# Two attention stages of a decoder kernel: context keys and values projected in parts, and self-attention on units of 256 queries

## The chip, the cores and the metric

The kernel runs on one core of a Trainium2 chip. The metric is the device time of one execution, in microseconds, the median of several runs.

## The reference

The computation is a stack of 12 blocks on x of shape (4 batches, 256 tokens, 128 channels). Two of them matter here.

The second context attention (layer 1): 16 heads of 8 channels, 256 queries per batch, keys and values projected from a context of 1601 places with 96 channels, a different one for each of the 4 batches. In float32: q = LN(x) Wq + bq, scaled by 8^-0.5; k = c Wk + bk; v = c Wv (its bias is added behind). The scores less their row maximum are clamped to +-10000, the softmax is over the 1601 places, and the result times Wo is added to x.

The non-causal self-attention inside layer 2's feed-forward block: a convolution over tokens, then 16 heads of 8 channels over the 256 tokens of a batch, softmax over all 256 keys, no mask.

## The kernel before, in words

Each stage of the program has one program of its own for each engine, ordered by hand; they meet on semaphores. The tensor engine takes its matmuls in program order. All arrays are float32, and each float32 matmul stands in the trace as two instructions. The 8 PSUM banks hold 512 float32 columns each.

**Second context attention** (`attend_clipped`, L1449; called from `layer1_context`, L1700). The work is cut into 16 units, a batch b and a group g of four heads, `X_UNITS` (L1387). A unit has 13 ticks, one for each tile of 128 context places (`JT`). For its queries a unit needs first the row maxima. `scan` (L1493) makes all scores in 11 bursts of three matmuls of 401 columns into banks 0 to 2; `reduce_` (L1640) on the vector engine takes the maxima of a burst. `prepare` (L1646) gathers and clamps them, `turn` (L1513) transposes them on the tensor engine into banks 0 and 1, and `add` (L1654) puts them into the queries. Then `fill` (L1519) makes the scores again, transposed and shifted, for a pair of ticks, in banks 3 to 6; ScalarE's `take` (L1586) makes the exponentials (L1611); `clip` (L1662) on the vector engine clips each tick against a floor; `values` (L1544) sums into bank 7, and ScalarE's `copy` (L1615) takes that out at the end of the unit.

The stage is pipelined over units (`SCAN_FROM`, L1390, and `bursts_in`, L1393). At ticks 0 to 5 of unit u the last six bursts of unit u + 1 are scanned and reduced, at ticks 8 to 12 the first five of unit u + 2. Ticks 6 and 7 have no burst. The vector engine gathers unit u + 1 at tick 6 and adds at tick 8 (L1677 to L1689); at tick 7 in the third unit of a batch it also sums the next context (`context_sum`, L1669).

Banks 3 to 6 are handed on by one chain of slots (`slots_in`, L1403; `X_SLOTS`). Each slot is filled by the tensor engine when ScalarE has taken the slot before (semaphores `filled` and `taken`). Slots are pairs, one floor per unit (tick 9), and, at tick 7 (`PREPARE_AT`) of the first two units of batches 0 to 2, the keys and the values of the next batch: four matmuls of up to 512 columns for keys (L1526), thirteen of 128 columns for values (L1529). ScalarE takes keys in one instruction into `k_rows` (L1594), values in two (L1601, L1602).

The queue of SP (L1471) spreads the keys by 16 DMAs from `k_rows` to `kT`, which is double-buffered by batch, and loads the contexts of batches 2 and 3. Its order is: two groups of the first keys, load 2, spread 1, load 3, spread 2, spread 3. Each waits for a count of `taken`, load also for the sum of an earlier context.

The order of the tensor engine at a tick, from the tick loop:

```python
for m in bursts_in(n):
    scan(m)
if i == PREPARE_AT and u + 1 < U:
    turn(u + 1)
for slot in slots_in(n):
    fill(slot)
if n == PAIRS[PAIR[n]][-1]:
    values(PAIR[n])
```

**Non-causal self-attention** (`self_attention`, L392, with causal=False, called at L2939). A unit is a batch, a group of four heads and one tile of 128 queries: 32 units. For each: `scan` (L438, four matmuls of 256 columns at L456, banks 0 to 3), `reduce` (L537, 1024 columns at L542), `turn` (L482, one transpose at L487, spare columns of bank 0), `shift` (L545, L552), `score` (L459, eight matmuls of 128 columns at L478, banks 4 to 7), one exponential of 1024 columns (L528), `values` (L490, eight matmuls of 128 columns at L496, spare columns of bank 4), and ScalarE's copy (L531). The order on the tensor engine is scan u + 1, score u, turn u + 1, values u. A scan waits for the shift of the unit before, a score for the copy of the unit before. The causal form of the same function, in other layers (L0a below is one), already has units of 256 queries, two exponentials of 768 columns per unit (L526), and the order score u, scan u + 2, turn u + 1, values u. When all units are through, 32 transposes (L516) and the division by the sums follow.

## Time and profile before

| | |
|---|---|
| median of 3 runs | 4305.74 us |
| lowest, highest | 4303.53, 4313.3 us |
| the profiled execution's own time | 4302.7 us |
| its span in the profile | 4301.0 us |
| mean granted TensorE clock | 0.873 of 2.4 GHz |
| tensor engine (PE) busy | 3334.1 us, 78% |
| vector engine (DVE) busy | 2990.1 us, 70% |
| ScalarE (ACT) busy | 1872.6 us, 44% |
| GpSimd (POOL) busy | 352.4 us, 8% |
| DMA queues | 5.1% of 16 engines' span |

The profile is of one execution, with times from the start of its span. A row of its timeline gives the start, the duration, the engine (PEld is the weight load of the tensor engine), the line of the kernel, the operation, what it writes and reads (partitions x elements), how many instructions were merged, and in brackets the idle time of the engine before it and what ended that. Busy shares over the whole span are means over many stages with different limits, so a stage is read by itself. The granted clock is a share of 2.4 GHz; 0.50 is 1.2 GHz.

### The profile page before, as it was taken

What the parts mean: (1) busy time and instruction counts of PE and PEld (TensorE: products, weight loads), DVE (VectorE), ACT (ScalarE), POOL (GpSimd) and SP (SyncE); (2) the same over time, 40 slices, a digit from 0 to 9 for tenths busy, and PEclk for the clock granted to TensorE, in tenths of its full rate; (3) what the DMA queues carried; (4) which work ended last, traced back from release to release, by engine and by line L of the source; (5) the groups of instructions that cost most, each with busy time, mean ns of one, the idle gap of its engine ahead of it and who ended that gap; (6) DMA issues with size and microseconds to landing.
All of it is one profiled execution on the core that took longest, in us unless ns stands there. A gap on an engine that the chain in (4) does not pass through costs nothing. (4 is left out here: it accounts for less than half of the span.)

```text
span 4301.0 us, 59641 instructions
## 1 busy us (share of the span) xinstructions
PE 3334.1 (78%) x24338; PEld 1735.1 (40%) x24338; DVE 2990.1 (70%) x4102; ACT 1872.6 (44%) x2168; POOL 352.4 (8%) x150
## 2 busy tenths in 40 slices
PE   5799999999999955877776884466654669477579
PEld 3433333333333324333334653223322347344357
DVE  4577777777777776699896446699998454546642
ACT  2365555565555532344442233344442236244233
POOL 0000000000000000000000000044441000000000
PEclk9899999999999978799997997666566789688789
DMA  2000000000000000100002001000000100010010
GB/s 83 9 15 8 8 15 8 8 13 10 8 8 15 1 12 13 22 8 8 9 1 94 30 2 47 1 0 0 0 0 0 41 11 30 9 40 1 1 41 6
DMA packets 21604, 68.51 MB, mean 16 GB/s; under 512 B 5201, under 2 KB 5713, under 8 KB 20434
## 3 DMA queue, kind: packets, MB, share of 16 engines
q1 hardware_dynamic: 21330, 64.69, 5.1%
q8 instruction: 193, 3.16, 0.3%
q14 instruction: 81, 0.66, 0.0%
HBM read 49.07 MB, written 0.52 MB: 12 GB/s over the span
## 5 line engine op out<-in xcount | busy, mean ns | idle before, releaser
L1071 PE MATMUL banks<-L0x_ring,L0x_context_rows 128*101 128x512 f32 x1600 | 734.7, 602 | 4.0 <-ACT L0x_ring L1119 4.0
L1130 ACT COPY L0x_ring<-banks 128x1024 f32<-128x1024 f32 (+1 forms) x416 | 387.1, 982 | 533.9 <-PE banks L1059 533.9
L1059 PE MATMUL banks<-L0x_q_thirds,L0x_context_thirds 32*128 32x512 f32 x4800 | 593.8, 606 | 10.3 <-DVE L0x_q_thirds L1236 5.3
L1161 DVE TENSOR_TENSOR L0x_ring<-L0x_ring,L0x_greatest 128x2048 f32<-128x2048 f32 (+1 forms) x208 | 469.9, 2268 | 10.9 <-ACT L0x_ring L1130 9.4
L1177 DVE TENSOR_TENSOR L0x_maxima<-L0x_maxima,L0x_ring 128x1024 f32<-128x1024 f32 (+1 forms) x288 | 322.8, 1162 | 201.1 <-ACT L0x_ring L1130 200.9
L1071 PEld LDWEIGHTS banks<-L0x_ring,L0x_context_rows 128*101 128x101 f32 x1600 | 253.9, 167 | 456.0 <-issue 448.9
L1119 ACT ACTIVATE L0x_ring<-L0x_ring 128x2048 f32<-128x2048 f32 (+1 forms) x208 | 386.4, 1858 | 16.6 <-DVE L0x_ring L1161 16.2
L1059 PEld LDWEIGHTS banks<-L0x_q_thirds,L0x_context_thirds 32*128 32x128 f32 x4800 | 237.1, 185 | 347.0 <-issue 306.7
L1611 ACT ACTIVATE L1x_probs<-banks 128x2048 f32<-128x2048 f32 (+1 forms) x112 | 196.6, 1755 | 252.6 <-PE banks L1540 210.8
L1644 DVE TENSOR_REDUCE L1x_maxima<-banks 128x3 f32<-128x1203 f32 (+1 forms) x176 | 241.3, 1372 | 54.1 <-PE banks L1509 54.1
L1667 DVE SCALAR_TENSOR_TENSOR L1x_probs<-L1x_probs,L1x_floor 128x1024 f32<-128x1024 f32 (+1 forms) x208 | 252.1, 1216 | 13.0 <-ACT L1x_probs L1611 13.0
L1509 PE MATMUL banks<-L1x_k,L1x_q 32*128 32x401 f32 x1024 | 176.8, 579 | 92.2 <-DVE L1x_maxima L1644 87.7
L1266 POOL PARTITION_ALL_REDUCE L0x_greatest<-L0x_folded_maxima x32 | 93.7, 2928 | 1388.5 <-DVE L0x_folded_maxima L1194 720.5
L3414 PE MATMUL banks<-L2x_k,L2x_q_of_head 128*128 128x512 f32 (+1 forms) x256 | 183.9, 813 | 0.0
L3519 DVE MAX8 L2x_top<-L2x_rest 128x8 f32<-128x1601 f32 x96 | 175.6, 1829 | 3.3
L3524 DVE MATCH_REPLACE8 L2x_rest<-L2x_top,L2x_rest 128x1601 f32<-128x1601 f32 x96 | 173.9, 1812 | 0.0
L1540 PE MATMUL banks<-L1x_q_shifted,L1x_k 32*128 32x256 f32 (+1 forms) x1664 | 169.7, 397 | 4.0 <-ACT L1x_probs L1611 4.0
L1177 DVE TENSOR_TENSOR L0x_maxima<-L0x_ring 128x1024 f32<-128x1024 f32 x64 | 75.6, 1222 | 97.1 <-ACT L0x_ring L1130 97.1
L3487 POOL TENSOR_TENSOR L2x_exp_all<-L2x_exp_all,L2x_exp_rest 128x1601 f32<-128x1601 f32 x31 | 110.9, 3577 | 258.6 <-ACT L2x_exp_top L3477 258.6
L1509 PEld LDWEIGHTS banks<-L1x_k,L1x_q 32*128 32x128 f32 x1024 | 56.8, 193 | 176.0 <-DVE L1x_maxima L1644 158.6
L1540 PEld LDWEIGHTS banks<-L1x_q_shifted,L1x_k 32*128 32x128 f32 (+1 forms) x1664 | 108.1, 185 | 35.5 <-ACT L1x_probs L1611 14.6
L250 PE MATMUL banks<-identity,z_rows 128*128 128x128 f32 x96 | 25.1, 438 | 125.1 <-DVE z_rows L285 123.7
(948 smaller groups left out, 5272.2 us busy)
## 6 DMA issues: line engine op xcount, KB each, us to landing
L0x_q_thirds<-L0x_q_context SPq DMA_DIRECT2D x180, 64.0 KB, 2.0
L1f_expert_weights<-in_L1f_experts SPq DMA_DIRECT2D x16, 512.0 KB, 10.0
L2f_expert_weights<-in_L2f_experts SPq DMA_DIRECT2D x8, 512.0 KB, 4.9
L3a_expert_weights<-in_L3a_experts SPq DMA_DIRECT2D x8, 512.0 KB, 5.6
L3f_expert_weights<-in_L3f_experts SPq DMA_DIRECT2D x8, 512.0 KB, 6.6
L1x_k<-L1x_k_rows SPq DMA_DIRECT2D x64, 50.0 KB
L0x_context_thirds<-in_context_thirds SPq DMA_DIRECT2D x1, 2496.0 KB, 14.3
L1x_context<-in_context SPq DMA_DIRECT2D x4, 600.4 KB, 4.7
```

Source lines behind the costliest of these rows:

```text
L1059: mm = pe.matmul(k.ps[:, score_bank(s) + i, :], thirds[group_rows(i), slot, t, :], q_thirds[group_rows(i), u // 2 % 2, t, :], start=t == 0 ...
L1071: mm = pe.matmul(k.ps[0:CW, bank, :], rows1[0:height(j), j, :], ring[0:height(j), s % RING, i, :], start=s == FIRST[u] and i == 0, stop=s ...
L1119: act.activation(ring[:, s % RING, 0:len(js), :], ring[:, s % RING, 0:len(js), :], ACT.Exp).then_inc(exped, 1)
L1130: act.copy(ring[0:r, s % RING, 2 * p:2 * p + len(pair), :], k.ps[0:r, bank:bank + len(pair), :]).then_inc(copied, 1)
L1161: dve.tensor_tensor(o, o, greatest[:, u % 2, None, :].broadcast_to([P, len(js), 512]), ALU.subtract).then_inc(shifted, 1)
L1177: dve.tensor_tensor(o, before, ring[0:r, s % RING, 2 * p:2 * p + m, :], ALU.max).then_inc(maxed, 1)
L1509: mm = pe.matmul(k.ps[:, bank + i, 0:WIDE], qT[row(h), g, b * S + it * P:b * S + (it + 1) * P], kT[row(h), b % 2, g, 400 * c:400 * c + WID ...
L1540: mm = pe.matmul(k.ps[0:height(j), 3 + h, i * S:(i + 1) * S], kT[row(h), b % 2, g, j * P:j * P + height(j)], qs[row(h), u % 2, :], start=T ...
L1611: act.activation(probs[0:r, at % 2, 0:m, :].rearrange("p a (h q) -> p h a q", h=4), k.ps[0:r, 3:7, 0:m * S].rearrange("p h (a q) -> p h a ...
L1644: dve.tensor_reduce(mx[:, u % 2, items[0]:items[-1] + 1], k.ps[:, scan_bank(m):scan_bank(m) + len(items), 0:WIDE], X, ALU.max).then_inc(re ...
L1667: dve.scalar_tensor_tensor(out=o, in0=o, scalar=1.0, in1=floor[0:height(j), u % 2, :], op0=ALU.min, op1=ALU.max).then_inc(clipped, 1)
L3414: mm = pe.matmul(k.ps[:, i, 0:m], qh[:, h, b * S + it * P:b * S + (it + 1) * P], kT[:, b % 2, c:c + m], start=False, stop=True)
```

## The change

It has two parts.

In the second context attention the slots of keys and values for batches 1 to 3 are gone. In their place each of the first 12 units has one part at tick 6: `part_ahead` on the tensor engine, into scan banks 1 and 2, and `take_part` on ScalarE. For the next batch, the first unit of a batch does the keys of places 0 to 801, the second those of 801 to 1600 (place 801 twice), the third the values of eight tiles, the fourth those of five. The part waits for all reductions of the next unit; the first scan of the next unit but one waits for `part_taken`. The turn now uses bank 0 alone. The gather stays at tick 6. SP's spread and load wait for counts of `part_taken`: the spread for the second part of a batch, load 3 for the fourth.

In layer 2 a new function, `attend_whole_batches`, takes the place of the non-causal call. Its units are 16, a batch and a group with all 256 queries. Exponentials are two of 1024 columns into a single buffer; a scan waits only for the reduction of the unit before, and the order on the tensor engine is that of the causal form.

The diff, cut where lines repeat what stands here:

```diff
+def attend_whole_batches(k, ctx_name, qT, kT, v, y, heads, dv):
+
+    groups = heads // 4
+    units = [(b, g) for b in range(B) for g in range(groups)]
+    U = len(units)
+    with ExitStack() as ctx:
+        low = k.sb(ctx_name + "_minus_max", [P, 2, TPB, P], ctx=ctx)
+        qs = k.sb(ctx_name + "_q_shifted", [P, 2, S], ctx=ctx)
+        probs = k.sb(ctx_name + "_probs", [P, 4, TPB * S], ctx=ctx)
+        yT = k.sb(ctx_name + "_y_columns", [P, TILES, groups, P], ctx=ctx)
+        rden = k.sb(ctx_name + "_reciprocal_sums", [P, TILES, heads], ctx=ctx)
+        with k.stage() as (block, signal):
...
+            @block.tensor
+            def _(pe):
+                def scan(u):
+                    if u:
+                        pe.wait_ge(reduced, u)
+                    for it in range(TPB):
+                        for h in range(4):
+                            mm = pe.matmul(k.ps[:, h, whole(it)], queries(u)[row(h), tile(it)], keys(u)[row(h)], start=True, stop=True)
+                    mm.then_inc(scanned, 1)
+
+                def turn(u):
+                    pe.wait_ge(reduced, u + 1)
+                    if u:
+                        pe.wait_ge(exped, 2 * u - 1)
+                    for it in range(TPB):
+                        mm = pe.transpose(k.ps[:, 6, tile(it)], low[:, u % 2, it, :], k.ident[:])
+                    mm.then_inc(turned, 1)
+
+                def score(u):
+                    pe.wait_ge(shifted, u + 1)
+                    if u:
+                        pe.wait_ge(copied, u)
+                    for j in range(TPB):
+                        for h in range(4):
+                            mm = pe.matmul(k.ps[:, 4 + h, whole(j)], keys(u)[row(h), tile(j)], qs[row(h), u % 2, :], start=True, stop=True)
+                    mm.then_inc(scored, 1)
+
+                def values(u):
+                    b, g = units[u]
+                    pe.wait_ge(exped, 2 * u + 2)
+                    for j in range(TPB):
+                        for h in range(4):
+                            mm = pe.matmul(k.ps[row(h), 4, 0:S], v[:, b * TPB + j, 4 * g + h, :], probs[:, h, whole(j)],
+                                           start=j == 0, stop=j == TPB - 1)
+                    mm.then_inc(summed, 1)
+
+                scan(0)
+                turn(0)
+                scan(1)
+                for u in range(U):
+                    score(u)
+                    if u + 2 < U:
+                        scan(u + 2)
+                    if u + 1 < U:
+                        turn(u + 1)
+                    values(u)
+                pe.wait_ge(copied, U)
...
+            @block.scalar
+            def _(act):
+                for u, (b, g) in enumerate(units):
+                    act.wait_ge(scored, u + 1)
+                    act.activation(probs[:, 2:4], k.ps[:, 6:8, :], ACT.Exp).then_inc(exped, 1)
+                    act.activation(probs[:, 0:2], k.ps[:, 4:6, :], ACT.Exp).then_inc(exped, 1)
+                    act.wait_ge(summed, u + 1)
+                    act.copy(yT[:, b * TPB:(b + 1) * TPB, g, :], k.ps[:, 4, 0:S].rearrange("p (t j) -> p t j", t=TPB)).then_inc(copied, 1)
+
+            @block.vector
...
+                def reduce(u):
+                    dve.wait_ge(scanned, u + 1)
+                    if u >= 2:
+                        dve.wait_ge(turned, u - 1)
+                    dve.tensor_reduce(low[:, u % 2, :, 31::32], k.ps[:, 0:4, :].rearrange("p h (i n) -> p i h n", i=TPB), X, ALU.max,
+                                      negate=True).then_inc(reduced, 1)
+
+                def shift(u):
+                    dve.wait_ge(turned, u + 1)
+                    if u >= 2:
+                        dve.wait_ge(scored, u - 1)
+                    dve.tensor_tensor(qs[:, u % 2, :], queries(u), k.ps[:, 6, 0:S], ALU.add).then_inc(shifted, 1)
+
+                reduce(0)
+                for u in range(U):
+                    shift(u)
+                    if u + 1 < U:
+                        reduce(u + 1)
...
@@ -1387,7 +1510,10 @@
 X_UNITS = [(b, g) for b in range(B) for g in range(4)]
 TICKS = JT * len(X_UNITS)
 NB = len(BURSTS)
-SCAN_FROM, GATHER_AT, PREPARE_AT, ADD_AT, FLOOR_AT = -5, 6, 7, 8, 9
+SCAN_FROM, PART_AT, GATHER_AT, PREPARE_AT, ADD_AT, FLOOR_AT = -5, 6, 6, 7, 8, 9
+PARTS_AHEAD = 4 * (B - 1)
+KEY_PARTS = ((0, 401), (801, 400))
+VALUE_PARTS = (range(0, 8), range(8, JT))
 
 
 def bursts_in(n):
@@ -1403,10 +1529,7 @@
 def slots_in(n):
 
     u, i = divmod(n, JT)
-    b, g = X_UNITS[u]
     out = []
-    if b + 1 < B and g < 2 and i == PREPARE_AT:
-        out.append(("values" if g else "keys", b + 1))
     if i == FLOOR_AT and u + 1 < len(X_UNITS):
         out.append(("floor", u + 1))
     out += [("pair", p) for p, tiles in enumerate(PAIRS) if tiles[0] == n + 2]
...
             def spread(b):
-                sp.wait_ge(taken, SLOT[("keys", b)] + 1)
+                sp.wait_ge(part_taken, 4 * (b - 1) + 2)
                 if b == 1:
...
             def load(b):
-                sp.wait_ge(taken, SLOT[("values", b - 2)] + 1)
+                if b == 2:
+                    sp.wait_ge(taken, SLOT[("values", 0)] + 1)
+                else:
+                    sp.wait_ge(part_taken, 4 * (b - 2))
                 sp.wait_ge(summed_context, b - 1)
                 sp.dma_start(context[:, b % 2, :], k.dram["context"][b]).then_inc(arrived[b], 16)
...
                 if burst == 0 and u:
                     pe.wait_ge(shifted, u)
+                if burst == 0 and 2 <= u < PARTS_AHEAD + 2:
+                    pe.wait_ge(part_taken, u - 1)
...
             def turn(u):
                 pe.wait_ge(clamped, u + 1)
                 for it in range(TPB):
-                    mm = pe.transpose(k.ps[:, it, 0:P], low[:, u % 2, it, :], k.ident[:])
+                    mm = pe.transpose(k.ps[:, 0, it * P:(it + 1) * P], low[:, u % 2, it, :], k.ident[:])
                 mm.then_inc(turned, 1)
+
+            def part_ahead(u):
+                b, g = X_UNITS[u]
+                pe.wait_ge(arrived[b + 1], 16)
+                pe.wait_ge(reduced, NB * (u + 2))
+                if g < 2:
+                    at, width = KEY_PARTS[g]
+                    for i in range(2):
+                        mm = pe.matmul(k.ps[:, 1 + i, 0:width], w["k"], context[:, (b + 1) % 2, at + i * width:at + (i + 1) * width],
+                                       start=True, stop=True)
+                else:
+                    for i, j in enumerate(VALUE_PARTS[g - 2]):
+                        mm = pe.matmul(k.ps[0:height(j), 1 + i // 4, i % 4 * P:(i % 4 + 1) * P],
+                                       context[:, (b + 1) % 2, j * P:j * P + height(j)], w["v"], start=True, stop=True)
+                mm.then_inc(part_made, 1)
 
...
@@ -1547,7 +1686,10 @@
                     b, g = X_UNITS[u]
                     pe.wait_ge(clipped, n + 1)
                     if j == 0:
-                        pe.wait_ge(taken, SLOT[("values", b)] + 1)
+                        if b:
+                            pe.wait_ge(part_taken, 4 * b)
+                        else:
+                            pe.wait_ge(taken, SLOT[("values", 0)] + 1)
                         if u:
                             pe.wait_ge(copied, u)
...
@@ -1573,6 +1715,8 @@
                     turn(u + 1)
                 for slot in slots_in(n):
                     fill(slot)
+                if i == PART_AT and u < PARTS_AHEAD:
+                    part_ahead(u)
                 if n == PAIRS[PAIR[n]][-1]:
                     values(PAIR[n])
             pe.wait_ge(copied, U)
...
+            def take_part(u):
+                b, g = X_UNITS[u]
+                at = b + 1
+                if g == 0:
+                    for i in range(G):
+                        act.wait_ge(first_keys.here[i], 64)
+                    if b:
+                        act.wait_ge(spread_keys, 16 * H * b)
+                if g == 2:
+                    if at == 1:
+                        act.wait_ge(cleared, 4)
+                    else:
+                        act.wait_ge(summed, PAIR[JT * G * (at - 1) - 1] + 1)
+                act.wait_ge(part_made, u + 1)
+                if g < 2:
+                    first, width = KEY_PARTS[g]
+                    act.activation(k_rows[:, first:first + 2 * width].rearrange("p (a n) -> p a n", a=2), k.ps[:, 1:3, 0:width],
+                                   ACT.Identity, bias=w["bk"]).then_inc(part_taken, 1)
+                elif g == 2:
+                    act.copy(v[:, at % 2, 0:8, :, 0:d], k.ps[:, 1:3, :].rearrange("p a (j h e) -> p (a j) h e", h=H, e=d)).then_inc(part_taken, 1)
+                else:
+                    act.copy(v[:, at % 2, 8:JT - 1, :, 0:d], k.ps[:, 1, :].rearrange("p (j h e) -> p j h e", h=H, e=d))
+                    act.copy(v[0:JLAST, at % 2, JT - 1, :, 0:d], k.ps[0:JLAST, 2, 0:P].rearrange("p (h e) -> p h e", h=H)).then_inc(part_taken, 1)
+
...
@@ -1657,7 +1817,7 @@
                 if u >= 2:
                     dve.wait_ge(taken, SLOT[("pair", PAIR[JT * (u - 1) - 1])] + 1)
                 dve.tensor_tensor(qs[:, u % 2, :].rearrange("p (t j) -> p t j", t=TPB),
-                                  qT[:, g, b * S:(b + 1) * S].rearrange("p (t j) -> p t j", t=TPB), k.ps[:, 0:TPB, 0:P], ALU.add).then_inc(shifted, 1)
+                                  qT[:, g, b * S:(b + 1) * S].rearrange("p (t j) -> p t j", t=TPB), k.ps[:, 0, 0:S].rearrange("p (t j) -> p t j", t=TPB), ALU.add).then_inc(shifted, 1)
...
@@ -2936,7 +3096,7 @@
-            self_attention(k, "L2f", q, kk, v, y, H, d, causal=False)
+            attend_whole_batches(k, "L2f", q, kk, v, y, H, d)
```

## Rows read from the trace of the kernel before

**Rows 1.** Windows, plain unit: length; PE, PEld, DVE, ACT, POOL busy; PEclk; DMA
```profile
1895.30:1926.00 30.70, 23.88 (x282) 11.76 (x282) 29.80 (x28) 14.29 (x16) 0.00 (x0) 1.00 0.01 1
```

**Rows 2.** Timeline, vector engine: the gathers that begin the prepare of each unit
```profile
1791.74 0.20 DVE L1648 TENSOR_REDUCE L1x_unit_maxima<-L1x_maxima 128x8 f32<-128x32 f32 x1
1828.13 0.20 DVE L1648 TENSOR_REDUCE L1x_unit_maxima<-L1x_maxima 128x8 f32<-128x32 f32 x1
1862.97 0.20 DVE L1648 TENSOR_REDUCE L1x_unit_maxima<-L1x_maxima 128x8 f32<-128x32 f32 x1
1895.26 0.20 DVE L1648 TENSOR_REDUCE L1x_unit_maxima<-L1x_maxima 128x8 f32<-128x32 f32 x1
1926.01 0.20 DVE L1648 TENSOR_REDUCE L1x_unit_maxima<-L1x_maxima 128x8 f32<-128x32 f32 x1
1960.69 0.20 DVE L1648 TENSOR_REDUCE L1x_unit_maxima<-L1x_maxima 128x8 f32<-128x32 f32 x1
1995.54 0.20 DVE L1648 TENSOR_REDUCE L1x_unit_maxima<-L1x_maxima 128x8 f32<-128x32 f32 x1
...
2029.43 0.20 DVE L1648 TENSOR_REDUCE L1x_unit_maxima<-L1x_maxima 128x8 f32<-128x32 f32 x1
...
2163.64 0.20 DVE L1648 TENSOR_REDUCE L1x_unit_maxima<-L1x_maxima 128x8 f32<-128x32 f32 x1
```

**Rows 3.** Timeline, all engines: a slot of keys (from 1928) and one of values
```profile
1928.07 3.01 PE L1526 MATMUL banks<-L1x_context,L_weights 96*128 96x512 f32 x8 [1.16 <-ACT L1x_probs L1611]
...
1931.01 1.06 PE L1554 MATMUL banks<-L1x_probs,L1x_v 128*16 128x256 f32 x16
1931.12 1.60 ACT L1594 ACTIVATE L1x_k_rows<-banks,L_weights 128x1601 f32<-128x1601 f32 x1 [3.10 <-PE banks L1526]
...
1933.00 1.41 DVE L1644 TENSOR_REDUCE L1x_maxima<-banks 128x3 f32<-128x1203 f32 x1 [3.73 <-PE banks L1509]
...
1962.76 3.16 PE L1529 MATMUL banks<-L_weights,L1x_context 96*128 96x128 f32 x26 [1.16 <-ACT L1x_probs L1611]
```

**Rows 4.** Timeline, all engines: ticks 6 to 8 of a plain unit
```profile
1894.08 1.15 PE L1540 MATMUL banks<-L1x_q_shifted,L1x_k 32*128 32x256 f32 x16
...
1895.30 1.88 ACT L1611 ACTIVATE L1x_probs<-banks 128x2048 f32<-128x2048 f32 x1 [1.68 <-PE banks L1540]
...
1895.72 0.44 PE L1516 MATMUL banks<-identity,L1x_minus_max 128*128 128x128 f32 x2 [0.49 <-DVE L1x_minus_max L1652]
...
1897.40 0.61 PE L1509 MATMUL banks<-L1x_k,L1x_q 32*128 32x401 f32 x3
...
1898.44 1.41 DVE L1644 TENSOR_REDUCE L1x_maxima<-banks 128x3 f32<-128x1203 f32 x1
```

**Rows 5.** Timeline, ScalarE: one unit of the non-causal loop at the full clock
```profile
3500.56 1.02 ACT L528 ACTIVATE L2f_probs<-banks 128x1024 f32<-128x1024 f32 x1 [0.93 <-PE banks L478]
...
3502.35 0.27 ACT L531 COPY L2f_y_columns<-banks 128x128 f32<-128x128 f32 x1 [0.76 <-PE banks L496]
...
3503.54 1.02 ACT L528 ACTIVATE L2f_probs<-banks 128x1024 f32<-128x1024 f32 x1 [0.93 <-PE banks L478]
```

**Rows 6.** Timeline, ScalarE: two exponentials of the same loop in its beginning
```profile
3417.57 1.02 ACT L528 ACTIVATE L2f_probs<-banks 128x1024 f32<-128x1024 f32 x1 [1.76 <-PE banks L478]
...
3421.81 1.02 ACT L528 ACTIVATE L2f_probs<-banks 128x1024 f32<-128x1024 f32 x1 [1.76 <-PE banks L478]
```

**Rows 7.** Timeline: exponentials, values and copy of one unit of a causal loop
```profile
81.08 1.51 ACT L526 ACTIVATE L0a_probs<-banks 128x768 f32<-128x768 f32 x2 [1.39 <-PE banks L474]
...
82.74 0.86 PE L496 MATMUL banks<-L0a_probs,L_v 128*32 128x128 f32 x24
...
83.67 0.37 ACT L531 COPY L0a_y_columns<-banks 128x256 f32<-128x256 f32 x1 [1.07 <-PE banks L496]
```

**Rows 8.** Windows: two stretches of the non-causal loop
```profile
3414.00:3418.00 4.00, 3.33 (x42) 2.25 (x41) 1.51 (x2) 1.04 (x3) 0.00 (x0) 0.50 0.00 0
...
3446.00:3458.00 12.00, 8.78 (x172) 5.57 (x164) 6.06 (x8) 5.16 (x8) 0.00 (x0) 1.00 0.01 2
```

52 lines of the change are left out of this document (33 added, 19 removed).

## The prediction

> **What bounds the kernel now.** I read the page first (the tensor engine is busy 78% of the span, the vector engine 70%), but the change touches only two stages, so the answer has to come from those. The second context attention runs from about 1735 to 2295 us, the loop of the non-causal self-attention from 3409 to 3512 us. For each I read the timeline of one repeating unit, then the same engines where the pattern breaks.
>
> In the second context attention a unit is 13 ticks. The windows view of a plain unit shows the vector engine busy 29.80 of 30.7 us at full granted clock [rows 1]: it bounds the plain unit. The start of the gather of maxima, one per unit, gives the period [rows 2]: 30.75 us plain (1895.26 to 1926.01), 32.29 where the sum of a context is taken (a 1.54 us longer unit), 36.39 and 34.68 with a projection of keys, 34.84 and 34.85 with one of values. So the projections are no longer covered: in such a slot the tensor engine waits for the exponentials, writes all four score banks for 3.0 to 3.2 us, ScalarE empties them, and only then the next pair and the next scan can start; the vector engine stands idle 3.73 us before a reduction [rows 3].
>
> In the self-attention no engine is full. The exponentials of neighbouring units start 2.98 us apart at the full clock [rows 5], and 4.24 us apart while the granted clock is 0.50 [rows 6, 8]. This is a ring: scores, exponential, values, copy, and the next scan and scores queued behind. The reader should see it in the 1.02 us exponential that fills only a third of the period.
>
> **Part 1, the projections leave the score banks.** Removed are six slots. Their price over a plain unit, from [rows 2]: 5.64 (36.39 - 30.75), 4.09, 3.93 and 4.10; for the last batch 2029.43 to 2163.64 is 134.21 us, less four plain units (123.00) and one context sum (1.54), leaves 9.67. Sum 27.43 us.
>
> Added are twelve parts, one in each of the first twelve units, at tick 6, behind the fill of the pair of ticks 8 and 9 and ahead of the turn of the next unit. In the plain unit that fill ends at 1895.23 and the turn starts at 1895.72 [rows 4]. The part also waits for the last reduction of the next unit; on the vector engine this lies ahead of a 1.2 us clip and of the gather at 1895.26, so it is over by 1894.1 and costs nothing. If it were late, the turn and the values of ticks 6 and 7 would be late behind it.
>
> A part of keys is 802 columns; 1601 take 3.01 us [rows 3], so 1.5 us. The turn then ends near 1897.2 instead of 1896.16, and the values of ticks 6 and 7 (0.98 us of issue) end near 1898.1. ScalarE is in the exponential until 1897.18 and its read-out until 1897.26 [rows 4], so the projection is done when it comes to it; 802 columns of its copy cost about 0.87 us (1.60 us for 1601 and 0.37 for 256 [rows 3, 7]). The banks are free at 1898.2, and the first scan of the next unit but one, queued behind, starts there and not at 1897.40: 0.8 us late, and the reduction of 1898.44, which had no wait, with it. A full vector engine cannot win that back. The second part of values (ten instructions of 26 that take 3.16 us, 1.2 us, then two short copies, 0.86 us) comes to 0.8 as well. The first part of values (1.9 us, a copy of about 1.1) falls into the unit in which the vector engine sums a context for 1.8 us at just this place; the next scan waits for that: 0, and 1.0 if the cover failed. That is 9 x 0.8 = 7.2 us. Bounds: nothing per part, or the whole of its projection and copy in a row (1.5 + 0.9 for keys; 1.9 + 1.1 and 1.2 + 0.9 for values: 9.9 a batch, 30 in all). I take 7.2 since the rows around it fix both starts. **Gain of part 1: 20.2 us**, from 27 to -3.
>
> Edits that cost nothing: both transposes of a turn go to one bank and the add reads one bank (same columns). The spread of keys leaves SP's queue a unit later than before; its 16 DMAs need about 11 us of issue, and the first scan that needs them comes a unit (31 us) after. Behind it on SP stand the load of context 3, now some 30 us later but wanted five units on, and the next spread. The cover for both is one unit; without it the first scan of a batch waits.
>
> **Part 2, units of 256 queries.** 32 units become 16. Tensor work is the same in columns: scan and scores are 16 instructions of 256 columns each, the form that takes 1.15 us for 16 [rows 4], values 16 at 1.06 [rows 3], the turn 0.44. The new ring, from the start of the scores: 1.21 to the first exponential (1894.08 to 1895.30); two exponentials of 1024, 1.95 us, as the causal loop runs two of 768 in 1.51, overlapping by 0.1 [rows 7]; 0.05 to values; 1.12 to the copy; 0.37 of copy; 0.1 to the next scores. 4.8 to 4.9, I take 4.85. The other ring, turn 0.44, add 0.4, reduction of 2048 (2.4, scaling 1.41 for 1203), scan 1.0, is about 4.3 and stays beneath. The next scan and turn (1.0 + 0.44 behind 1.0 of scores) end 0.5 us before the exponentials, so values do not wait for them. What was late, the copy, is still last.
>
> Two old units cost 5.96, so each new one saves 1.11. In the half-rate stretch (14 us in the old run) the tensor engine bounds the new ring: scores 2.2, scan 2.2, turn 0.7, values 2.1, copy and handoffs 0.5 make 7.7 against 8.48. 14 x 1.11 + 2 x 0.8 = 17.1. The pipeline fills later: the first reduction is 1.1 us longer and two scans 0.4 to 0.5 each: -2. **Gain of part 2: 15 us.** Bounds, against 32 x 2.98 = 95 us: if nothing but ScalarE's own 2.4 us a unit counted, 38, a gain of 57; if nothing overlapped (scores 1.2, scan 1.2, reduction 2.4, turn 0.5, exponentials 2.0, values 1.1, copy 0.4 = 8.8), 141, a loss of 46. The causal loop is nearest: it starts its first values 1.66 us after its first exponential [rows 7], as my ring supposes, so I stay near it, with 9 to 19.
>
> Sum: 4302.7 (the profiled execution's own time, of which the span is 4301.0) - 20.2 - 15 = 4267.5. The median shown is 3.0 above that execution, the fastest run 0.8. For a run I forecast 4269.
>
> **Rivals.**
> - *The tick-6 block doesn't hide* (0.12). Part 1 costs the serial 2.4 us each instead of 0.8. For it: the vector engine has only 0.9 us of slack in a unit [rows 1]. Against: ScalarE had been idle 1.68 us before the exponential of that tick [rows 4], so it is the engine with room. Gain 27 - 30 + 15: 4291.
> - *The self-attention ring does not shorten* (0.08): the second exponential or the reduction of 2048 holds the scores, period near 6. Against: the reduction ends 2 us before it is wanted. Gain 20 alone: 4283.
> - *The clock, and the kernel gets slower* (0.03). While the granted clock was 0.50 the tensor engine was busy 3.33 of 4 us, at 1.00 it is 8.78 of 12 [rows 8]; so the rate is not a matter of that share alone, and I can't say from the rows what sets it. Were the new ring to stay at 1.2 GHz, its units take 7.7: 16 x 2.85 = 46 us more than forecast. If each part in the context attention were to take a half-rate stretch too (1.7 us, as the first projection, 36.39 against 34.68 [rows 2]), 20 more: 4335. It decides from a dozen of such units on, or six with the parts. Against: the busy share in the new ring is 3.7 of 4.85, above the old.
> - *It does not do what it says* (0.02): the projections or spreads come late and the first scan of a batch waits, about 10 us a batch: 4299.
>
> On the clock the Trainium skill ("TensorE: Matmul & The Clock Gate", Part 1) says that the slow rate is the default and that activity releases it, and its section on HAM oscillation that waits inside a loop bring it back. By that the longer waits for 256-query exponentials speak against this change. The trace of before keeps 1.00 through a loop with waits of its own, and no run here shows the new one yet.
>
> **From cases to numbers.** The forecast has 0.75. Its own range is 4258 to 4281 (20 - 5 and + 6; 15 - 6 and + 4, not all at once). To leave out no more than 2 in 10 it reaches to the second rival and some of the first: 4257 to 4286. About 0.2% (8.6 us) is what a measurement of this kernel can tell from no change. Faster by more: 0.75 + 0.12 + 0.08 = 0.95. Within: 0.02. Slower: 0.03.
>
> **What would show it.** In the changed profile the gathers of units with parts should be 31.5 us apart, 32.3 in those with a context sum, 30.75 behind the twelfth; no reduction there waits over 1.5 us. ScalarE's part copies start straight behind the read-out of an exponential. In the self-attention the first of two exponentials returns every 4.85 us, and the loop ends about 3477 instead of 3512, 20 of the 35 us being earlier gain. I am wrong if part units are over 32.5, if the ring is over 5.5, or if the granted clock is 0.50 in the middle of either stage.

## The result, and the profile after

The median went from 4305.02 us (4303.53 to 4313.3, four runs) to **4269.13 us** (4262.95 to 4270.59, four runs); the ratio, estimated apart from the medians, is 0.9908, with a 95% interval of 0.9897 to 0.992. The two medians are 35.9 us apart; the ratio stands for 39.6, its interval for 34 to 44. In the experiments below, one of six runs of the kernel with 128-query units in the new order took 4388.35 us at a mean granted clock of 0.832, where its others had 0.872 to 0.875; it counts in the median given there, not in the ratio. The profiled execution took 4270.48 us, of which the span is 4268.6; before these were 4302.7 and 4301.0. From the page after, the busy time of each engine:

```profile
PE 3312.7 (78%) x23817; PEld 1723.8 (40%) x23826; DVE 2984.5 (70%) x4070; ACT 1868.6 (44%) x2158; POOL 352.4 (8%) x150
```

The shares are those of before. The change shows only in the two stages, and the two traces balance. The context attention, from the start of the first context sum to the start of the vector engine's copy of the next norm's columns, took 584.4 us before and 563.1 now: 21.3 us. The self-attention, from the clearing of its minus-max buffer to its last reciprocal, took 108.4 and takes 92.8: 15.6 us. In between, code that nobody touched took 2.6 us more, ahead of the first stage 2.0 more: 36.9 less 4.6 is 32.3 of the 32.4 us between the spans.

**The context attention.** Timeline of the vector engine after: the gathers that begin the prepare of each unit, as [rows 2] show them before.

```profile
1793.68 0.20 DVE L1808 TENSOR_REDUCE L1x_unit_maxima<-L1x_maxima 128x8 f32<-128x32 f32 x1
1825.37 0.20 DVE L1808 TENSOR_REDUCE L1x_unit_maxima<-L1x_maxima 128x8 f32<-128x32 f32 x1
1857.06 0.20 DVE L1808 TENSOR_REDUCE L1x_unit_maxima<-L1x_maxima 128x8 f32<-128x32 f32 x1
1889.35 0.20 DVE L1808 TENSOR_REDUCE L1x_unit_maxima<-L1x_maxima 128x8 f32<-128x32 f32 x1
1920.69 0.20 DVE L1808 TENSOR_REDUCE L1x_unit_maxima<-L1x_maxima 128x8 f32<-128x32 f32 x1
1952.22 0.20 DVE L1808 TENSOR_REDUCE L1x_unit_maxima<-L1x_maxima 128x8 f32<-128x32 f32 x1
...
2174.09 0.20 DVE L1808 TENSOR_REDUCE L1x_unit_maxima<-L1x_maxima 128x8 f32<-128x32 f32 x1
2204.85 0.20 DVE L1808 TENSOR_REDUCE L1x_unit_maxima<-L1x_maxima 128x8 f32<-128x32 f32 x1
```

The differences are 31.69, 31.69, 32.29, 31.34, 31.53 us and, behind the twelfth part, 30.76. The units of 34.7 to 36.5 us are gone. The twelve units with parts took 402.65 us before and take 380.41 (1793.68 to 2174.09). Over a plain unit the parts cost 0.94 twice in the first batch and 0.78 twice in the two others (keys), 0.59 in each fourth unit, and nothing beside a context sum: 6.8 us.

Not all of the 22.2 us is what the slots themselves cost. In the kernel before the granted clock fell to 0.50 for 3.4 us in three of these twelve units; in the kernel after it fell in none. Two of the three were units with a slot, as the timeline of before shows (compare the 3.01 and 3.16 us in [rows 3]):

```profile
1793.80 4.71 PE L1526 MATMUL banks<-L1x_context,L_weights 96*128 96x512 f32 x8 [1.16 <-ACT L1x_probs L1611]
...
2096.93 4.80 PE L1529 MATMUL banks<-L_weights,L1x_context 96*128 96x128 f32 x26 [1.15 <-ACT L1x_probs L1611]
```

The units around them took 36.39 us against 34.68 for the other unit with keys, and 36.48 against 34.85 for the other one with values. The third fall is in the unit of 33.89 us, 1.60 over its like. Together that is 4.9 us, so 17.3 of the 22.2 us stand without the clock.

Timeline after, all engines, ticks 6 and 7 of a unit with a part of keys, as [rows 4] show a plain one before:

```profile
1920.59 1.62 PE L1654 MATMUL banks<-L1x_context,L_weights 96*128 96x401 f32 x4
1920.73 1.88 ACT L1745 ACTIVATE L1x_probs<-banks 128x2048 f32<-128x2048 f32 x1 [1.69 <-PE banks L1679]
...
1922.05 0.38 PE L1644 MATMUL banks<-identity,L1x_minus_max 128*128 128x128 f32 x2
1922.36 1.06 PE L1696 MATMUL banks<-L1x_probs,L1x_v 128*16 128x256 f32 x16
...
1922.60 0.92 ACT L1765 ACTIVATE L1x_k_rows<-banks,L_weights 128x802 f32<-128x802 f32 x1
1923.62 0.61 PE L1637 MATMUL banks<-L1x_k,L1x_q 32*128 32x401 f32 x3 [0.20 <-issue]
...
1924.62 1.41 DVE L1804 TENSOR_REDUCE L1x_maxima<-banks 128x3 f32<-128x1203 f32 x1 [0.59 <-PE banks L1637]
```

Read it from below. The reduction waited 0.59 us, where it had no wait before, since its scan starts at 1923.62. Two things end there nearly together: the values, issued from 1922.36 on, and ScalarE's copy of the part, which ends at 1923.52. The copy starts with no idle time of ScalarE ahead of it: the projection was done at 1922.21, 0.4 us before.

**The self-attention.** Timeline after, one unit at the full clock; [rows 5] are its counterpart.

```profile
3409.57 1.15 PE L626 MATMUL banks<-L2f_q_shifted,L2f_k 32*128 32x256 f32 x16 [0.58 <-ACT L2f_y_columns L661]
3410.51 1.07 PE L609 MATMUL banks<-L2f_k,L2f_q 32*128 32x256 f32 x16
3410.77 1.02 ACT L658 ACTIVATE L2f_probs<-banks 128x1024 f32<-128x1024 f32 x1 [1.35 <-PE banks L626]
3411.69 1.02 ACT L659 ACTIVATE L2f_probs<-banks 128x1024 f32<-128x1024 f32 x1
...
3412.76 1.07 PE L634 MATMUL banks<-L2f_probs,L2f_v 128*32 128x256 f32 x16 [0.41 <-ACT L2f_probs L659]
3413.90 0.37 ACT L661 COPY L2f_y_columns<-banks 128x256 f32<-128x256 f32 x1 [1.19 <-PE banks L634]
3414.42 1.15 PE L626 MATMUL banks<-L2f_q_shifted,L2f_k 32*128 32x256 f32 x16 [0.58 <-ACT L2f_y_columns L661]
```

The scores return every 4.85 us (3409.57 to 3414.42), and each step is released by the one above it: scores, two exponentials, values, copy, scores. Windows of the same loop after (columns as in [rows 1]):

```profile
3400.00:3404.00 4.00, 4.00 (x34) 1.74 (x30) 1.61 (x2) 0.94 (x2) 0.00 (x0) 0.51 0.00 0
3408.00:3470.00 62.00, 44.01 (x632) 28.17 (x632) 33.64 (x25) 29.14 (x39) 0.00 (x0) 1.00 0.01 2
3474.00:3479.00 5.00, 2.63 (x24) 0.60 (x16) 0.00 (x0) 2.19 (x3) 0.00 (x0) 0.50 0.00 0
```

The granted clock is 0.50 in the first unit and the last, whose periods are 6.92 and 5.79 us, and 1.00 for the 62 us between. The Trainium skill ("TensorE: Matmul & The Clock Gate", HAM oscillation) warns that waits inside a loop, in its case for a DMA in every pass, bring the slow rate back. This trace doesn't bear that out for a ring that idles in spots of 0.4 to 0.6 us and is busy 44 of 62 us.

### The profile page after: what moved, and what is told of

It reads as the page before. It is cut to its first block and busy times, and to the rows that moved or that the text cites. A ratio compares the mean times of both kernels' runs of the same rounds, so it can differ in the third digit from the quotient of the medians.

```text
span 4268.6 us, 58517 instructions
## 1 busy us (share of the span) xinstructions
PE 3312.7 (78%) x23817; PEld 1723.8 (40%) x23826; DVE 2984.5 (70%) x4070; ACT 1868.6 (44%) x2158; POOL 352.4 (8%) x150
## 5 line engine op out<-in xcount | busy, mean ns | idle before, releaser
L1637 PE MATMUL banks<-L1x_k,L1x_q 32*128 32x401 f32 x1024 | 176.0, 577 | 92.8 <-DVE L1x_maxima L1804 88.9
```

Of the source, the lines that this page charges most:

```text
L1637: mm = pe.matmul(k.ps[:, bank + i, 0:WIDE], qT[row(h), g, b * S + it * P:b * S + (it + 1) * P], kT[row(h), b % 2, g, 400 * c:400 * c + WID ...
```

## The experiments

Each was compared with the kernel before on its own chip; the medians of before were 4306.47 for the first four, 4305.02 for the doubled copies, the doubled projections, the tiny parts and the divided wait for the copy, and 4305.09 for the other three. Ratios have their 95% interval behind them.

**Each part alone.** Part 1 without part 2, from the kernel after:

```diff
-        attend_whole_batches(k, "L2f", q, kk, v, y, H, d)
+        self_attention(k, "L2f", q, kk, v, y, H, d, causal=False)
```

> The context attention changed, the non-causal self-attention as before (32 units, 2.98 us apart). Theory (two separate gains that add): the stage from the first context sum to the columns of the next norm is 21.3 us shorter, as in the changed kernel, so 4305.0 - 21 = 4284, within 3 us. Rival (most of the gain sits in the self-attention): above 4295. The parts cost 0.6 to 0.9 us each where no context is summed, the gathers stand 31.3 to 31.7 us apart.

Measured: 4283.98, 0.9949 (0.9937 to 0.9961), the context stage 563.2 us, its gathers within 0.01 us of those after. Part 2 without part 1, from the kernel before, with the new function added:

```diff
-        self_attention(k, "L2f", q, kk, v, y, H, d, causal=False)
+        attend_whole_batches(k, "L2f", q, kk, v, y, H, d)
```

> Only the self-attention on units of 256 queries; the context attention as before. Theory: its stage from first scan to the next columns is 109.1 us before and 93.5 in the changed kernel, so 4305.0 - 15.5 = 4289.5, within 3 us; ring 4.85 us. Rival (the two parts don't add, because the granted clock after one depends on the other): e1 and e2 together are more than 4 us off 35.9 us of gain.

Measured: 4289.7, 0.9965 (0.9953 to 0.9977). Its self-attention stage took 88.8 us and had the same period of 4.85 (on 88.8 against 92.8 see the last section). By the ratios the parts are worth 22 and 15 us, 37 together, against 40 for the whole by its ratio; by the medians they are worth 22.5 and 16.8, 39 together, against 36. Each ratio is uncertain by about 5 us to either side, so the totals show only that the parts add up within some 5 us. The firmer sign that neither needs the other is in the stages: the same gathers and the same ring with and without the other part.

**Size or order.** The new loop has larger units and also another order. Larger units, the order of before:

```diff
-                scan(1)
                 for u in range(U):
+                    if u + 1 < U:
+                        scan(u + 1)
                     score(u)
-                    if u + 2 < U:
-                        scan(u + 2)
```

> The changed kernel, but its 16 units in the old order on the tensor engine: scan u+1 ahead of score u. Theory (the size of the unit gives the gain, the order a part): the scan (1.0 us) now stands between values and scores, where only 0.5 us of copy and handoff was: ring 5.35 us, 8 us slower than the changed kernel, 4277. Rival (the order is what gives the gain, the size nothing): ring 5.96, 4287. Third (the scan is covered anyway): 4269.

Measured: 4273.48, 0.9927 (0.9916 to 0.9939). Timeline of this kernel, one unit:

```profile
3412.03 1.02 ACT L657 ACTIVATE L2f_probs<-banks 128x1024 f32<-128x1024 f32 x1 [1.57 <-PE banks L626]
...
3413.52 0.44 PE L617 MATMUL banks<-identity,L2f_minus_max 128*128 128x128 f32 x2 [1.55 <-DVE L2f_minus_max L671]
...
3415.03 1.15 PE L609 MATMUL banks<-L2f_k,L2f_q 32*128 32x256 f32 x16
3415.16 0.37 ACT L660 COPY L2f_y_columns<-banks 128x256 f32<-128x256 f32 x1 [1.19 <-PE banks L634]
3415.99 1.04 PE L626 MATMUL banks<-L2f_q_shifted,L2f_k 32*128 32x256 f32 x16
```

The scan ahead of the scores costs little, because ScalarE's copy (3415.16) runs under it: the period is 5.07 us, not the 5.35 expected. From the copy to the scores it is 0.83 us here and 0.52 in the kernel after (3413.90 to 3414.42). The other way round, 32 units of 128 queries in the new order; each exponential of 1024 columns is split into two of 512, too:

```diff
-    turn_bank = 6 if causal else 0
-    pairs = ((6, 2), (4, 0)) if causal else ()
+    turn_bank = 6
+    pairs = ((6, 2), (4, 0))
...
-                    if not causal and u + 1 < len(units):
-                        scan(u + 1)
                     score(u)
-                    if causal and u + 2 < len(units):
+                    if u + 2 < len(units):
                         scan(u + 2)
...
```

> The context attention changed; the self-attention keeps 32 units of 128 queries but takes the new order: scan two units ahead behind the scores, turn in bank 6, two exponentials of 512. Theory (size): the old ring is exponential, values, copy, scores and their handoffs; the reordering takes nothing from it and a second exponential adds 0.1: 3.0 to 3.1 us a unit, 4284 to 4288, as e1 or little above. Rival (order): the scan leaves the ring, 2.5 us a unit, 4269.

Measured: 4285.05, 0.9954 (0.9941 to 0.9966), nothing on top of part 1 alone. Timeline of this kernel:

```profile
3450.41 1.09 ACT L520 ACTIVATE L2f_probs<-banks 128x512 f32<-128x512 f32 x2 [0.93 <-PE banks L475]
...
3453.45 1.09 ACT L520 ACTIVATE L2f_probs<-banks 128x512 f32<-128x512 f32 x2 [0.93 <-PE banks L475]
```

3.04 us for a small unit, where the old order has 2.98; the second exponential accounts for 0.07 of it (1.09 us for the pair, 1.02 for one). From the copy to the scores it is 0.41 us in both orders (here 3449.21 to 3449.62). So size gives the gain: 5.07 against 5.96 for two small units in the old order is 0.89 of the 1.11 us, and the new order gives the other 0.22. It has nothing to give to the small unit, whose scan of 0.71 us is nearly through when the copy ends; the large one's takes 1.15.

Where the size gains can be read by setting two rings of before against one of after. The scores and values of before, timeline:

```profile
3501.64 0.65 PE L496 MATMUL banks<-L2f_probs,L2f_v 128*32 128x128 f32 x16
...
3502.76 0.73 PE L478 MATMUL banks<-L2f_q_shifted,L2f_k 32*128 32x128 f32 x16
```

With [rows 5], twice the small ring is 1.56 us from scores to exponential, 2.16 from there to the values, 1.42 to the copy and 0.82 to the scores; the large ring has 1.20, 1.99, 1.14 and 0.52. No single handoff makes the 1.11 us: the four stretches give 0.36, 0.17, 0.28 and 0.30.

**What a part costs, and through what.** If ScalarE's copy sets the scan behind a part, doubling the copy shows at full size; if the projection is hidden, doubling it shows only in part. ScalarE's copies doubled (the first of two goes to columns that nobody reads yet):

```diff
                     first, width = KEY_PARTS[g]
+                    act.activation(yT[:, 6:8].rearrange("p t g n -> p (t g n)")[:, 0:2 * width].rearrange("p (a n) -> p a n", a=2),
+                                   k.ps[:, 1:3, 0:width], ACT.Identity, bias=w["bk"])
...
                 elif g == 2:
+                    act.copy(yT[:, 6:8].rearrange("p t g n -> p t (g n)"), k.ps[:, 1:3, :])
...
                 else:
+                    act.copy(yT[:, 6].rearrange("p g n -> p (g n)"), k.ps[:, 1, :])
```

> The changed kernel with ScalarE's copy of each part out of the scan banks made twice (the first into space that nothing reads yet). It prices ScalarE's share of the path to the first scan. Theory: in units with keys the scan starts 0.1 to 0.2 us behind the end of the copy, so nearly all of a second one (0.92) shows, 0.85 x 6; in the fourth unit of a batch 0.55 x 3; in the third, with the context sum, 0.6 of the 1.0 is covered, 0.4 x 3: 8 us slower than the changed kernel, 4277. Rival (the tensor engine alone sets the scan): within 2 us of it, 4269 to 4271.

Measured: 4278.18, 0.993 (0.9918 to 0.9943). Timeline of this kernel, tick 7 of a key unit:

```profile
1923.16 0.92 ACT L1765 ACTIVATE L1x_y_columns<-banks,L_weights 128x802 f32<-128x802 f32 x1
...
1923.97 0.93 ACT L1767 ACTIVATE L1x_k_rows<-banks,L_weights 128x802 f32<-128x802 f32 x1
...
1925.00 0.61 PE L1637 MATMUL banks<-L1x_k,L1x_q 32*128 32x401 f32 x3 [1.02 <-issue]
...
1925.99 1.41 DVE L1808 TENSOR_REDUCE L1x_maxima<-banks 128x3 f32<-128x1203 f32 x1 [1.41 <-PE banks L1637]
```

The second copy starts 0.81 us after the first, and the key unit is 0.82 us longer (32.51 against 31.69). The tensor engine now stands idle for 1.02 us ahead of the scan, instead of 0.20; the trace names no releaser, but the second copy ends at 1924.90, 0.1 us before. Over the twelve units the gathers give 7.9 us, as expected. The total alone would not have told theory from rival: the five runs lie between 4271.73 and 4280.94, and the profiled one is the 4271.73. Then the projections doubled:

```diff
-                    for i in range(2):
+                    for i in (0, 1, 0, 1):
...
-                    for i, j in enumerate(VALUE_PARTS[g - 2]):
+                    for i, j in 2 * list(enumerate(VALUE_PARTS[g - 2])):
```

> The changed kernel with the matmuls of each part made twice. Theory: what stands behind them on the tensor engine (turn, values of ticks 6 and 7, first scan) comes later by nearly the whole: 1.3 x 6 for keys, 0.9 x 3 and, in the unit with the context sum, 1.9 less 0.55 of cover, 1.35 x 3: 14.5 us slower than the changed kernel, 4283.5. Rival (only ScalarE's copy sets the scan, the tensor engine has room): 0 to 3 us, 4269 to 4272.

Measured: 4284.24, 0.9948 (0.9936 to 0.9961). Timeline of this kernel:

```profile
1930.05 2.96 PE L1654 MATMUL banks<-L1x_context,L_weights 96*128 96x401 f32 x8
...
1932.85 0.38 PE L1644 MATMUL banks<-identity,L1x_minus_max 128*128 128x128 f32 x2
1933.13 0.93 ACT L1765 ACTIVATE L1x_k_rows<-banks,L_weights 128x802 f32<-128x802 f32 x1 [0.98 <-PE banks L1654]
```

The turn starts 2.71 us behind the gather (1930.14), against 1.36 in the kernel after. Of these 1.35 us the key units show 1.09 and 0.99, the fourth unit 0.79; beside the context sum it is 1.42. Only the first 0.3 us or so are covered; the copy now waits 0.98 us for the projection. So thin is the cover of part 1. Over the twelve units it is 13.0 us, for 14.5 expected. Both costs taken away, with the waits kept (the projection of the later batches is left out):

```diff
-                if g < 2:
-                    at, width = KEY_PARTS[g]
...
+                mm = pe.matmul(k.ps[:, 1, 0:8], w["k"], context[:, (b + 1) % 2, 0:8], start=True, stop=True)
...
+                act.activation(yT[:, 7, 3, 0:8], k.ps[:, 1, 0:8], ACT.Identity, bias=w["bk"]).then_inc(part_taken, 1)
```

> The changed kernel with each part shrunk to one matmul of 8 columns and a copy of 8 columns; the projection of keys and values for batches 1 to 3 is left out, all waits stay. It is the floor of the parts. Theory: the nine parts that cost 0.6 to 0.9 us (6.8 us by the gathers of the changed kernel) go to 0.1: 6 us faster than the changed kernel, 4263; gathers 30.8 to 30.9 us apart. Rival (the 0.7 us are handoffs that any part costs): within 1.5 us of it, 4268 to 4269.

Measured: 4269.5, 0.9917 (0.9903 to 0.993), 6 us over the expectation and level with the kernel after, as the rival had it, although the gathers came as expected: 31.02 or 31.03 us in the first key units and 30.87 later, 5.4 us less in sum. One unit with a context sum took 35.94 us instead of 32.29. That is 3.65 of the missing 6 us in this one execution, which at 4266.47 us was the fastest of the five; where the median lost the rest isn't shown. Windows of this kernel at that place:

```profile
1986.00:1987.20 1.20, 0.00 (x1) 0.03 (x1) 1.20 (x3) 0.00 (x0) 0.00 (x0) 0.86 0.00 0
1987.00:1997.00 10.00, 9.24 (x60) 4.38 (x63) 6.32 (x6) 3.08 (x3) 0.00 (x0) 0.50 0.01 2
```

And its timeline there:

```profile
1987.20 1.05 PE L1637 MATMUL banks<-L1x_k,L1x_q 32*128 32x401 f32 x3 [1.47 <-DVE L1x_q_shifted L1803]
...
1997.39 1.41 DVE L1788 TENSOR_REDUCE L1x_maxima<-banks 128x3 f32<-128x1203 f32 x1 [2.65 <-PE banks L1637]
```

The tensor engine stood idle for 1.47 us while the vector engine summed a context. Still in this idle spot, at 1986.9, the granted clock fell to 0.50 for 10.2 us, and the scans came late. Before has this too, for 3.4 us, in its unit of 33.89 us [rows 2]. Windows of before, around the end of that idle spot:

```profile
1998.00:1999.20 1.20, 0.00 (x0) 0.01 (x1) 1.20 (x3) 0.00 (x0) 0.00 (x0) 0.97 0.00 0
1999.20:2001.50 2.30, 2.27 (x16) 1.74 (x19) 1.58 (x2) 0.00 (x0) 0.00 (x0) 0.50 0.00 0
```

**The clock at the context sum.** In the kernel after, the first part of values works in just that idle spot. So put only this back into the kernel with tiny parts:

```diff
+                if g == 2:
+                    for i, j in enumerate(VALUE_PARTS[0]):
+                        pe.matmul(k.ps[:, 1 + i // 4, i % 4 * P:(i % 4 + 1) * P],
+                                  context[:, (b + 1) % 2, j * P:(j + 1) * P], w["v"], start=True, stop=True)
                 mm = pe.matmul(k.ps[:, 1, 0:8], w["k"], context[:, (b + 1) % 2, 0:8], start=True, stop=True)
```

> The kernel with tiny parts, but the third unit of a batch has its eight matmuls back (their copy and the other projections stay left out). In three kernels whose tensor engine stands idle 1.5 us in the tick of the context sum (before, the one with the self-attention alone, the tiny parts) the granted clock fell there in 4 of 9 such units, and they took 1.1 to 3.7 us longer than 32.29; in the six with matmuls there, in none of 18. Theory (this work keeps the clock up): all three such units 32.3 us, and the median 1 to 3 us under that of the tiny parts. Rival (the falls are chance): at least one of the three at 33 us or more, about as likely as not, and the median the same.

Measured: 4263.35, 0.9902 (0.9889 to 0.9916), and all three such units at 32.28 or 32.29, as the theory has it. The median is 6 us under that of the tiny parts, where 1 to 3 were expected, but on another chip and with overlapping intervals, and the two profiled executions differ by only 0.6 us in span (4264.2 against 4264.8). So the units are the evidence here, not the total. (The expectation counts six kernels and 18 units; there were seven by then, with 21 units.) And into the kernel before, eight matmuls that nobody reads:

```diff
                 if n == PAIRS[PAIR[n]][-1]:
                     values(PAIR[n])
+                if i == PREPARE_AT and u % 4 == 2 and u // 4 + 1 < B:
+                    for j in range(8):
+                        pe.matmul(k.ps[:, 2, j % 4 * P:(j % 4 + 1) * P], pick[:], k.ident[:], start=True, stop=True)
```

> The kernel before, with eight matmuls that nobody reads put into the tick of the context sum (behind the values of ticks 6 and 7). Nothing waits for them but the next scan, for which the tensor engine had 1.5 us to wait. Theory as in the run above: no fall of the clock in these units, 32.3 us each, but up to 0.4 us more if the filling is longer than the wait; median 0 to 3 us below the kernel before. Rival: one of the three units at 33.4 us or more, as in the kernel before.

Measured: 4304.75, 0.9998 (0.9989 to 1.0007). No unit with a context sum at 0.50, but the filling takes 2.05 us where 1.5 were idle and puts 0.45 us on each of the three units (32.74), so nothing is won: the null result says neither yes nor no to a gain that the 1.35 us of filling would have eaten. Over all profiled executions: in the kernels that leave the tensor engine idle there (before, part 2 alone, tiny parts) 4 of 9 such units had a stretch at 0.50 and took 1.1 to 3.7 us more; in those with work there none of 30. The context sum is not what matters: the slots of before, each behind an idle spot of 1.16 us, had such a stretch in 5 of 18 (before, part 2 alone, before with the filling), while in the ten kernels that have parts in place of slots only the one unit of 35.94 us had one among these twelve. That work in the idle spot prevents the fall is well supported, but each kernel was profiled once, and for any one unit chance is not excluded. What sets the clock stays open: 5 of 9 idle spots of 1.47 us and 13 of 18 of 1.16 had no fall. The Trainium skill's rule cited above, that waits in a loop bring the slow rate back, agrees in direction with the units that fell.

**Where the part stands.** Behind the turn at tick 7 instead of ahead of it:

```diff
-                if i == PART_AT and u < PARTS_AHEAD:
+                if i == PART_AT + 1 and u < PARTS_AHEAD:
                     part_ahead(u)
```

> The changed kernel with each part one tick later on the tensor engine, behind the turn of tick 7 and ahead of the values. Theory (the values of ticks 6 and 7 and ScalarE's copy both stand ahead of the scan, nearly level; the turn doesn't matter): the part now ends 0.9 us later than before, so the copy does, of which 0.45 us shows in units with keys and 0.25 in those with a context sum: gathers 31.8 to 32.1 in units with keys, 32.5 with the context sum, 3 to 4 us in all, 4272 to 4273. Rival (it was the late turn and add that cost the 0.6 to 0.9 us): gathers 31.0 to 31.1, 4264.

Measured: 4272.34, 0.9927 (0.9914 to 0.9939); gathers 32.16, 32.08, 32.65, 31.55 us apart, 4.3 us more in all. Timeline of this kernel:

```profile
1923.44 0.93 ACT L1765 ACTIVATE L1x_k_rows<-banks,L_weights 128x802 f32<-128x802 f32 x1 [0.37 <-PE banks L1654]
...
1925.47 1.41 DVE L1804 TENSOR_REDUCE L1x_maxima<-banks 128x3 f32<-128x1203 f32 x1 [1.14 <-PE banks L1637]
```

Now ScalarE waits 0.37 us for the projection, and the reduction 1.14 instead of 0.59. Ahead of the turn is the better place, by 0.2 to 0.5 us a unit.

**The step that the ring has left.** The copy holds bank 4 alone, the scores of heads 1 to 3 go to banks 5 to 7. So only head 0 waits for the copy:

```diff
-                    if u:
-                        pe.wait_ge(copied, u)
-                    for j in range(TPB):
-                        for h in range(4):
-                            mm = pe.matmul(...)
-                    mm.then_inc(scored, 1)
+                    for heads_now in ((2, 3, 1), (0,)):
+                        if heads_now == (0,) and u:
+                            pe.wait_ge(copied, u)
+                        for j in range(TPB):
+                            for h in heads_now:
+                                mm = pe.matmul(...)
+                        mm.then_inc(scored, 1)
...
-                    act.wait_ge(scored, u + 1)
+                    act.wait_ge(scored, 2 * u + 1)
                     act.activation(probs[:, 2:4], k.ps[:, 6:8, :], ACT.Exp).then_inc(exped, 1)
+                    act.wait_ge(scored, 2 * u + 2)
...
-                        dve.wait_ge(scored, u - 1)
+                        dve.wait_ge(scored, 2 * u - 2)
```

> The changed kernel, but the scores of heads 1 to 3 no longer wait for ScalarE's copy out of bank 4, only those of head 0 do, and they are signalled in two, so that the exponential of heads 2 and 3 can start before those of head 0 are there. Theory (the ring runs through the copy): the first exponential follows the values by about 1.15 us and not by 1.75: ring 4.25 to 4.35 us for 4.85, 8 us faster, 4261. Rival (the other ring, turn, add, reduction, scan, 4.2 to 4.4 us by its rows, or the order behind the scores takes over at once): 4.7 to 4.85, 4267 to 4269.

Measured: **4259.63**, 0.9892 (0.9879 to 0.9906). Timeline of this kernel:

```profile
3432.85 2.29 DVE L674 TENSOR_REDUCE L2f_minus_max<-banks 128x8 f32<-128x2048 f32 x1
3433.53 1.69 PE L627 MATMUL banks<-L2f_q_shifted,L2f_k 32*128 32x256 f32 x16
3433.67 0.37 ACT L663 COPY L2f_y_columns<-banks 128x256 f32<-128x256 f32 x1 [1.19 <-PE banks L635]
3434.72 1.03 ACT L659 ACTIVATE L2f_probs<-banks 128x1024 f32<-128x1024 f32 x1 [0.69 <-PE banks L627]
3435.19 1.15 PE L609 MATMUL banks<-L2f_k,L2f_q 32*128 32x256 f32 x16
...
3436.27 0.44 PE L617 MATMUL banks<-identity,L2f_minus_max 128*128 128x128 f32 x2
...
3437.08 2.29 DVE L674 TENSOR_REDUCE L2f_minus_max<-banks 128x8 f32<-128x2048 f32 x1
```

The scores start at 3433.53, ahead of the copy; the first exponential waits 0.69 us instead of 1.35. The period is 4.19 to 4.23 us. The reductions are 4.23 apart (3432.85 to 3437.08), and this is the other ring of the prediction, put there at about 4.3: from reduction to scan 2.34 us, from scan to turn 1.08, from turn by way of the add to the next reduction 0.81. The self-attention stage takes 82.8 us, 10.0 less than after (in both the granted clock was 0.50 in the first and the last unit), and the median is 9.5 under it, though in another set of runs, and the intervals of the two ratios overlap by a little: the stage is the firmer evidence.

## Why the prediction was right

**The whole.** Forecast 4269 in a range of 4257 to 4286; measured 4269.13. Part 1 was put at 20.2 us and gave 22.2 between the gathers (21.3 over the stage: the code behind the last gather took 63.4 us before and 64.3 after, and 64.4 and 64.6 in the two experiments made from the kernel before); part 2 at 15 and gave 15.6. The stretches outside, which moved by 4.6 us the other way, show how much of so close a hit is luck. For the profiled execution itself the sum was 4267.5, and it took 4270.5.

**Removed slots.** 27.43 us, as read from [rows 2]. There was 1.60 us more to get in that execution: the unit of 33.89 us (1995.54 to 2029.43) has no slot in it, so I left it out of the sum, though it stands 1.60 over the other context-sum unit of 32.29. That excess is a stretch at 1.2 GHz, which did not come in the kernel after. And the 27.43 us hold two more such stretches, 1.70 us in the first unit with keys and 1.63 in the last with values, so the slots by themselves cost 24.1. The prediction had seen the first of these as a danger of the change and priced both as if a slot always cost them; in the two experiments that keep the slots, four and one of the first twelve units had a stretch at 0.50, not always the same ones. Set against those two the same gathers of the kernel after give 23.4 us and, less the filling, 19.0, so the 22.2 hang in part on the execution of before.

**Added parts.** 9 x 0.8 = 7.2 us forecast, 6.8 measured, and nothing beside the context sums, as forecast. The steps are in the rows: the turn ends at 1922.43, 1.74 us behind the gather (I had put it at 1.9), the copy has 0.92 us for 802 columns (0.87), the scan starts 2.93 us behind the gather, where [rows 4] had 2.14: 0.8 later. What I called the end of the chain, ScalarE's copy, is a near tie with the values: doubling it cost its full 0.82 us, doubling the projection all but 0.3.

**Part 2.** The ring at 4.85 us came out as 4.85, term by term: 1.20 to the first exponential (3409.57 to 3410.77), 1.94 for both, 0.05, 1.14 from values to copy, 0.37 and 0.15. At half rate I expected 7.7 us and two such units; there was one of 6.92 and one of 5.79. In the first the scan (2.09 us), turn (0.69) and values (1.85) came near their terms, but the clock was back before the next scores, which took 1.15 and not 2.2. The last has no scan and turn left in it; only its scores were slow (2.09). Sum of the fifteen periods after: 6.92 + 13 x 4.85 + 5.79 = 75.8. Thirty-one before: 3 x 4.25 + 28 x 2.98 = 96.2, of which one has no counterpart: 17.4 us gained, for 17.1 forecast. The stage gained 15.6, which leaves 1.8 for the filling, for 2 forecast; this is a difference, not measured by itself. It also sets a long stage of after against a long one of before; in the short ones (88.8 and 104.2 us, last section) the gain is 15.4, but a long one of after against a short one of before would show 11.4.

**The rivals.** The block at tick 6 hides: the serial 2.4 us would have given units of 33.2, and the unit that comes nearest to them is that with doubled projections, 32.8. The self-attention ring shortened, and size did it, not the order. The clock didn't turn against the change; in three units it turned in its favour, by 4.9 us. The spreads came in time: the first scan that reads new keys starts at 1860.75, in the tick behind the sum of the next context, and what it waits for (0.53 us) is the vector engine's add; SP had issued the last of the 16 DMAs at 1838.9, and the unit takes 32.29 us as it does before.

## What to carry to other kernels

When an engine's work is moved out of a full hand-over chain into another, price it by the scan, load or reduction queued behind its new banks, and look for the unit in which that one waits anyway: there the work is free. A ring of short steps on three engines pays its handoffs, and what each group of instructions costs beyond its columns, once per unit, so a larger unit gains what they cost, and the next gain is in splitting the wait of its longest link by bank. Ask of an idle spot of the tensor engine not only what it wastes but what the clock does behind it.

## What the runs showed of the hardware that was not expected

- **1.2 to 1.5 us of idle time on TensorE, and the granted clock 0.50 from somewhere between 0.4 us ahead of its end and 1.2 us behind it,** for 3.4 us in eight units and 10.2 in one, out of 29 units with such a spot, in a stage where it is otherwise busy 23.88 of 30.70 us [rows 1]. The kernel with 256-query units in the old order, which leaves TensorE idle 1.55 us ahead of each turn, had this in the middle of its loop, too: four stretches of 3.4 us at 0.50, in four units of 6.6 to 6.8 us instead of 5.07; the eight units before them were undisturbed. The new order, with 0.36 us there, had none in the middle of the loop in any of its seven profiles. Window of the kernel in the old order, 256-query units:

```profile
3448.00:3456.00 8.00, 6.24 (x62) 3.75 (x58) 4.03 (x3) 2.35 (x4) 0.00 (x0) 0.73 0.00 0
```

- **Two lengths of the same loop.** The new self-attention stage took either 92.8 us (after and three experiments) or 88.8 (three others), with no difference in its code: in the long ones the first unit has 6.9 to 7.0 us and the last 5.8, in the short ones 5.5 and 4.85. It is the clock: in the long ones it is 0.50 for 6.8 us in the first unit and again from the last one on (3400 to 3404 and 3474 to 3479 in the windows of after above), in the short ones for 3.4 us in the first unit and then only behind the loop. The old loop shows the same: 108.4 twice, 104.2 once. The unchanged code between the two stages took 1089.7 us in before, about 1090.5 in six other profiles and 1092.3 in six. Identical code ahead of the first stage ended between 1734.7 and 1741.9 us. So executions of one kernel differ by several us, in steps, and of a gain of 10 us the stage tells more than the total.
- **256 columns for less than twice 128.** The 16 score matmuls take 1.15 us at 256 columns and 0.73 at 128 (in the kernel of 128-query units in the new order), the reduction 2.29 against 1.23. That, too, is in the gain of the larger unit.
